# First attention of two transformer blocks: the weighing by the values in two halves of the queries, with a longer ring of exponentials

## What is computed

```python
q = _rope(proj(Wq, bq))
k = _rope(proj(Wk, bk))
v = proj(Wv, bv)
scores = jnp.einsum('bhtd,bhsd->bhts', q, k) / scale
attn = jax.nn.softmax(scores, axis=-1)
out = jnp.einsum('bhts,bhsd->bhtd', attn, v)
...
x = x + _layernorm(_L0_attn_ref(_layernorm(x, axis=-1), ...), axis=-1)
x = x + _layernorm(_L0_ffn_ref(_layernorm(x, axis=-1), ...), axis=-1)
```

## Time and profile before

| | us |
|---|---|
| median of 3 runs | 3386.52 (3385.89 to 3389.96) |
| the profiled execution | 3379.02 |
| its span, first to last instruction | 3377.2 |
| the first attention, in the span | 238 to 1638 |

### The profile page before, as it was taken

How to read it: one execution, slowest core, us unless ns; L and a number is a source line. 1 busy time by engine, 2 the same in 40 slices (tenths; PEclk the granted TensorE clock), 3 DMA queues, 4 the chain that set the end, 5 groups by cost and what they waited for, 6 DMA issues and landing times. The chain is left out here.

```text
span 3377.2 us, 56295 instructions
## 1 busy us (share of the span) xinstructions
PE 3182.4 (94%) x20728; PEld 2050.2 (61%) x20792; DVE 2572.0 (76%) x4114; ACT 2144.2 (63%) x4870; POOL 764.8 (23%) x954
## 2 busy tenths in 40 slices
PE   8979999999999999999859999999999999999996
PEld 5633333333333333333448888888888888888885
DVE  4578888888888888886357777777777777777774
ACT  3417777777777777777745555555555556565563
POOL 4500000000000000000343333333334343343341
PEclk9959999999999999999979999999999999999998
DMA  3322222222222222222400000000000000000001
GB/s 116 129 50 39 39 38 38 38 38 38 38 38 38 34 36 32 33 38 29 144 32 1 1 0 0 0 0 0 0 1 34 1 0 0 0 0 0 0 1 68
DMA packets 47027, 97.95 MB, mean 29 GB/s; under 512 B 17184, under 2 KB 29472, under 8 KB 40480
## 3 DMA queue, kind: packets, MB, share of 16 engines
q1 hardware_dynamic: 42400, 95.48, 15.1%
q10 hardware_dynamic: 4544, 1.38, 0.2%
HBM read 71.13 MB, written 25.69 MB: 29 GB/s over the span
## 5 line engine op out<-in xcount | busy, mean ns | idle before, releaser
L653 DVE TENSOR_REDUCE mx<-aux 128x1 f32<-128x1024 f32 x1024 | 1203.6, 1219 | 169.0 <-PE aux L528 168.8
L623 ACT ACTIVATE probs<-scores 128x512 f32<-128x512 f32 x2048 | 1062.9, 604 | 312.1 <-PE scores L552 308.9
L528 PE MATMUL aux<-k_stack,q_stack 48*128 48x512 f32 x2048 | 815.1, 476 | 31.6 <-DMA k_stack<-qk_dram 18.2
L552 PE MATMUL scores<-q_stack,k_stack 50*128 50x512 f32 x2048 | 756.4, 450 | 50.7 <-ACT probs L623 24.6
L552 PEld LDWEIGHTS scores<-q_stack,k_stack 50*128 50x128 f32 x2048 | 342.7, 186 | 602.6 <-ACT probs L623 549.6
L563 PE MATMUL pv<-probs,v_ones 128*32 128x512 f32 x4096 | 551.3, 610 | 1.4 <-ACT probs L623 0.7
L528 PEld LDWEIGHTS aux<-k_stack,q_stack 48*128 48x128 f32 x2048 | 345.3, 191 | 132.9 <-DVE mx L653 68.6
L1186 PE MATMUL bank<-QO,w_sb 128*128 128x128 f32 x2816 | 333.5, 278 | 0.9 <-ACT QO L1267 0.9
L1186 PEld LDWEIGHTS bank<-QO,w_sb 128*128 128x128 f32 x2816 | 321.3, 193 | 12.1 <-issue 10.3
L494 POOL CAST m_parts<-head_max 128x16 fp32r<-128x16 f32 x32 | 6.3, 196 | 1370.8 <-DVE head_max L658 1370.8
L1199 PE MATMUL bank<-kT,wqkv_sb 64*128 64x128 f32 x1984 | 288.6, 285 | 9.5 <-issue 0.4
(11 more groups left out here) (172 smaller groups left out, 4667.7 us busy)
## 6 DMA issues: line engine op xcount, KB each, us to landing
q_stack<-qk_dram SPq DMA_DIRECT2D x192, 128.0 KB, 5.0
k_stack<-qk_dram SPq DMA_DIRECT2D x192, 128.0 KB, 6.9
qk_dram<-qkT_hi SPq DMA_DIRECT2D x32, 256.0 KB, 3.1
qk_dram<-qkT_lo SPq DMA_DIRECT2D x32, 256.0 KB, 3.6
out<-x_sb SPq DMA_DIRECT2D x9, 384.0 KB, 4.1
wqkv_sb<-in_wqkv SPq DMA_DIRECT2D x2, 1536.0 KB, 7.4
w_sb<-in_w SPq DMA_DIRECT2D x2, 1408.0 KB, 11.3
x_sb<-in_x SPq DMA_DIRECT2D x1, 2048.0 KB, 18.8
```

What stands on the lines that cost most here:

```text
L528: last = nc.tensor.matmul(aux[:, ring["unit"], block_of_keys % 2], q_stack[rows, r % BODY, tile * P:(tile + 1) * P], k_stack[rows, r % BOD ...
L552: nc.tensor.matmul(scores[:, item % BANKS1], k_stack[0:SCORE_ROWS, r % BODY, s * P:(s + 1) * P], q_stack[0:SCORE_ROWS, r % BODY, j * 512:( ...
L623: nc.scalar.activation(probs[:, item % PROBS], scores[:, item % BANKS1], ACT.Exp, scale=float(D1) ** -0.5).then_inc(probs_ready, 1)
L653: nc.vector.reduce_max(mx[:, slot, tile, half:half + 1], aux[:, unit].rearrange("p a k -> p (a k)"), AX.X).then_inc(max_taken, 1)
```

## The change

`weigh` gets a half: it does the first or the last 256 queries of each block in all four matmuls, and both halves add up in the same bank. `weigh_earlier` picks the step that is meant. In a step, at j = 0 the second half of the step before last is weighed, and at j = 2 the first half of the last step, so a half stands behind every second pair. In step 1 the first half comes at j = 3 instead, since the copy of `pv` has to be done. `pv_done` rises with the second half. The ring `probs` has 12 blocks instead of 8, and the exponentials wait for the weighing three steps back. ScalarE's copy of `pv` moves behind its first exponential of step 1, because the last half of a head is now weighed at j = 0 of that step.

```diff
--- before.py
+++ after.py
@@ -337,9 +337,10 @@
 BLOCKS = T // 512
 BANKS1 = 3
 UNITS = 2
-PROBS = 8
+PROBS = 3 * BLOCKS
 BODY = 3
 VW = 32
+HALF = 256
 LEAD = 5
 AHEAD = BLOCKS * (TB + LEAD) - 1
 LOADS = 6
@@ -552,17 +553,27 @@
                 nc.tensor.matmul(scores[:, item % BANKS1], k_stack[0:SCORE_ROWS, r % BODY, s * P:(s + 1) * P],
                                  q_stack[0:SCORE_ROWS, r % BODY, j * 512:(j + 1) * 512], start=True, stop=True).then_inc(scores_ready, 1)
 
-            def weigh(r, s):
+            def weigh(r, s, half):
 
                 if s == 0:
                     pe.wait_ge(v_made, r + 1)
                     if r:
                         pe.wait_ge(pv_copied, r)
                 pe.wait_ge(probs_ready, BLOCKS * (TB * r + s + 1))
+                columns = slice(half * HALF, (half + 1) * HALF)
                 for j in range(BLOCKS):
-                    last = nc.tensor.matmul(pv[VW * j:VW * (j + 1), :], v_ones[:, r % BODY, s, :], probs[:, (BLOCKS * s + j) % PROBS],
-                                            start=(s == 0), stop=(s == TB - 1), tile_position=(0, VW * j))
-                last.then_inc(pv_done, 1)
+                    last = nc.tensor.matmul(pv[VW * j:VW * (j + 1), columns], v_ones[:, r % BODY, s, :], probs[:, (BLOCKS * (TB * r + s) + j) % PROBS, columns],
+                                            start=(s == 0 and half == 0), stop=(s == TB - 1 and half == 1), skip_group_check=True, tile_position=(0, VW * j))
+                if half == 1:
+                    last.then_inc(pv_done, 1)
+
+            def weigh_earlier(r, d, s, back, half, left, first):
+
+                if s >= back:
+                    if left >= d:
+                        weigh(r + d, s - back, half)
+                elif not first:
+                    weigh(r + d - 1, TB + s - back, half)
 
             def output_item(r):
 
@@ -581,10 +592,10 @@
                     a, tile, block_of_keys = max_item(d, s, j)
                     if left >= a:
                         score_for_max(r + a, tile, block_of_keys, head_begun if (d, s, j) == (0, LEAD, 1) else None)
-                    if j == 2 and s == 0 and not first:
-                        weigh(r + d - 1, TB - 1)
-                    elif j == 2 and s and left >= d:
-                        weigh(r + d, s - 1)
+                    if j == 0:
+                        weigh_earlier(r, d, s, 2, 1, left, first)
+                    if j == (3 if s == 1 else 2):
+                        weigh_earlier(r, d, s, 1, 0, left, first)
                     if j == 2 and (d, s) == (0, ROWS_STEP) and left >= 1:
                         maximum_rows(r + 1)
                     if j == 2 and (d, s) == (1, OUT_STEP) and not first:
@@ -618,16 +629,16 @@
             def exponentiate(r, s, j):
                 item = BLOCKS * (TB * r + s) + j
                 act.wait_ge(scores_ready, item + 1)
-                if j == 0 and TB * r + s >= 2:
-                    act.wait_ge(pv_done, TB * r + s - 1)
+                if j == 0 and item >= PROBS:
+                    act.wait_ge(pv_done, TB * r + s - PROBS // BLOCKS + 1)
                 nc.scalar.activation(probs[:, item % PROBS], scores[:, item % BANKS1], ACT.Exp, scale=float(D1) ** -0.5).then_inc(probs_ready, 1)
 
             def head(r, n, left):
                 for d, s in steps():
-                    if (d, s) == (1, 1):
-                        act.wait_ge(pv_done, TB * (r + 1))
-                        nc.scalar.copy(o_stage[:], pv[:]).then_inc(pv_copied, 1)
                     for j in range(BLOCKS):
+                        if (d, s, j) == (1, 1, 1):
+                            act.wait_ge(pv_done, TB * (r + 1))
+                            nc.scalar.copy(o_stage[:], pv[:]).then_inc(pv_copied, 1)
                         if (d, s, j) == (0, ROWS_STEP, 3) and left >= 1:
                             place = [what[3] for what in aux_items(left)].index("rows")
                             copy_rows(r + 1, (first_unit(left) + place) % UNITS)
```

## The result

| | us |
|---|---|
| before, median of 4 runs | 3386.81 (3385.89 to 3389.96) |
| changed, median of 4 runs | 3434.61 (3426.62 to 3469.98) |
| ratio | 1.016 (95% interval 1.0086 to 1.0234) |
| profiled execution, before and changed | 3379.02 and 3442.48 |

The change made the kernel slower by 1.6%, where 1.2% faster was forecast. Its runs differ by 43 us among themselves, those of before by 4 here, and by 26 in the 16 runs beside the first experiments. One run of one experiment (eight halved steps, 3526.9 us) fell into the chip's slower state and is left out of its median and ratio.

The account below looks back on a forecast made before the run. PE was taken as the pace-setter, stalled for score banks while ScalarE idled during weighings. Terms 74 + 3 - 18 - 3 - 8 - 6 - 3 gave 39 us off: 3340 profiled, 3347 median, range 3312 to 3386.

Parts of the forecast that it names:

- The regular step: Four score pairs and one weighing in the first attention: 2.61 us to become 2.46, 74 us off over 512 steps.
- the bound of PE: In the regular step after the change PE sets the pace at 2.46 us; VectorE needs 2.35, ScalarE 2.07.
- the gone wait for ScalarE: Fourth score pair held 0.39 us until ScalarE frees a score bank; this wait was to vanish.
- neither 0.50 nor 0.71: Bounds on half a weighing until the next pair: 0.50 with nothing fixed, 0.71 with the fixed part doubled; 0.57 taken.
- Rows of maxima: Step 13 of a head: maximum matmul behind the transpose waits for VectorE; +0.85 us a head, 18 us back in all.
- output: Step 3 of the next head, with the output transposes: next half +0.84 us, 3 us back in all.
- switch of heads: Step 1, where the copy of pv waits for the last half: +0.37 us, 8 us back in all.
- plain head: A head without a loop's end: 42.9 us before, forecast 41.4 after.
- The 3 us off for VectorE's end of a head: The 0.1 us left over per head before, which 0.4 us of slack should take in: 3 us off.
- The end of the loop: Every third head, the sequencer lowers the semaphores: +1.40 us before, 2.0 taken after, 6 us back over ten ends.
- The clock: Stretches at 1.2 instead of 2.4 GHz after a loop's end cost more: 3 us charged, bounds 0 and 24.
- the rival: Clock falls at each loop's end: 24 us instead of 3, giving 3368 us; chance 8%.

Follow-up runs that it names:

- the first experiments: The follow-ups told first: the changed kernel with its 32 heads written out instead of a loop, 3321.08 us; the kernel before, likewise written out, 3360.16 us.
- eight halved steps: Changed kernel in its loop, weighings of steps 3 to 10 in halves, the other eight whole, about 1982 PE instructions a turn: 3461.24 us, ratio 1.0258.
- 1694: Changed kernel in its loop, weighings of steps 6 and 7 alone in halves, about 1694 PE instructions a turn: 3364.77 us, ratio 0.9935.
- 1790: Changed kernel in its loop, weighings of steps 5 to 8 in halves, the other twelve whole, about 1790 PE instructions a turn: 3437.48 us, ratio 1.0173.
- 1646: Changed kernel in its loop, weighing of step 7 alone in halves, about 1646 PE instructions a turn: 3381.32 us, ratio 0.9999.
- loop of six heads: Kernel before, whole weighings, six heads in a turn of the loop instead of three: 3397.54 us, ratio 1.004.
- loop of 15 heads: Changed kernel, all in halves, 15 heads in a turn, so two turns and one branch back: 3341.92 us, ratio 0.9887.

## Why the prediction was wrong

The range, 3312 to 3386, did not hold 3434.61, and the sign was wrong. By its own steps:

- **The regular step**: right. 2 x (0.34 + 0.32 + 0.57) = 2.46 is in the trace, and the bound of PE, and the gone wait for ScalarE. The half cost its 0.57, neither 0.50 nor 0.71. With 1.00 for the whole, that leaves 0.14 in each that does not shrink with the columns. The Trainium skill (TensorEngine Tiling (Array Packing), Key Properties) says that a change of the tiling mode drains the engine; the trace agrees in so far as every half pays the 0.14, but no run separates a drain from other fixed costs. The multiplication was off: 512 x 0.15 is 77, not 74. The steps measure 2.609 and 2.463, which is 75, so it did no harm.
- **Rows of maxima, output, switch of heads**: right, +0.85, +0.84 and +0.38 (2.84 less 2.46), against +0.85, +0.84 and +0.37. A plain head took 41.5, 41.4 was forecast.
- **The 3 us off for VectorE's end of a head**: wrong. In the trace the step with the last item of a head is 0 to 0.45 us longer than 2.46 in a plain head, 0.1 in the mean, so the slack does not take it in. The plain heads take 41.6 in the mean, not 41.4, which makes about 7 us over 32 heads; the 41.5 of the head above is one of the shorter ones.
- **The end of the loop**: this is the step that failed. I priced it from the 3.12 us of before, as work of the sequencer that halves cover less, at 2.0, which is 6 us more for all ten. The branch back takes 3.4 to 3.9 us instead of 0.21, over the nine 30.5 us more, since a turn of 2369 PE instructions is not kept and 1598 were.
- **The clock**: the mechanism was named, its size was not. 3 us were charged, and 24 in the rival, by one step after each end. PE now idles 4.9 to 5.5 us at a taken branch where it idled 1.6, and the granted clock falls within each of these idle times and stays down for 7 to 41 us; with 7 us at the tenth end it is 181 us of the stage after its start. A half follows a half in 2.16 us there instead of 1.23. The nine ends with a taken branch took together 113 us more than plain heads; 18 of that is the 2.0 forecast, 30.5 the branches, and the 64 left is the clock.

The sum closes to a few us: the stage took from its first score to the last weighing 1400.3 us before and 1452.9 after, +52.6, where -39 was forecast, 91.6 apart. The branches are 30.5 of it. The clock cost 64 at the nine ends and about 3 at the tenth, but before had paid for it too (24 us at the lower level, 8 us by the heads that they lie in) and 3 more were charged, so it is 56. The 5 left are of the size of the plain heads' 7. Another 8 us of the profiled execution lie ahead of the stage, where both kernels run the same instructions; the start of the stage lies between 228 and 245 us in the twelve traces, in no order with the changes.

Two things in the profile should have led here. The count of PE's instructions per turn was in the prediction (32 to 48 per step), but only as a rate, never as a length. And after the first turn of the loop the trace of before has no instruction packets in the loop at all: the body is kept, so its length has a limit that the change could cross. The Trainium skill has the rule, and I did not weigh it: Runtime: NRT & Kernel Launch, Instruction fetch mechanics, says that instructions are fetched in blocks of 16 KB, in sequence, that PE's memory for them holds 2048, and that a taken branch to a target outside the current window of two blocks waits for a fetch. The traces agree on the block (155 packets, 2.54 MB) and on the wait, with the packet inside each long branch. They do not agree on the window of two blocks: before branches back over 1598 instructions in 0.21 us, without a fetch. And the limit in a loop was lower than 2048: 1694 were kept, 1790 and 1982 were not. In the first turn the kernels with 1598, 1646 and 1694 fetched seven blocks, those with 1790 and 1982 eight; so what is kept may be seven blocks of 256, an estimate from these counts that no run tests closer.

The large spread of the runs fits: how long the clock stays down differs from end to end (7 to 41 us in one execution). What decides it stays open. With whole weighings it was 7 to 14 (four ends in a loop of six heads), with halves over 20 at 15 of 28 ends; no run separates the reasons.

## What to carry to other kernels

Before you add instructions to a loop's body, count those of each engine per turn, and look in the profile whether instructions are fetched inside the loop at all: if not, the body is kept, and there is a length at which that ends. The loss then is not at the changed instructions but at the branch back, and a busy PE pays for the stall again in clock, here twice as much (64 us against 30.5). Where a forecast is right for every instruction and still misses, look at what happens once per turn; and taking the loop away is a quick way to see it: here the halves gain 39 us without the loop and lose 48 within it.

## What the runs showed of the hardware

- PE's sequencer kept a loop body of 1598, 1646 and 1694 instructions over ten turns without a fetch after the first, but not one of 1790, 1982, 2369 or 3179. The branch back took 0.21 us in the first three and 3.3 to 3.9 in the others, and in the loop of 15 heads (11777). One packet of instructions lay inside each of these 32 long branches, and ended 1.3 to 1.5 us before the branch did.
- Straight code of over 20000 PE instructions in the stage was fetched without a visible cost, at 24 matmuls and weight loads in 1.23 us: the regular step is 2.46 us written out as in the loop, and with whole weighings 2.61 in both.
- Within each of the 32 idle times of PE at these branches, 4.8 to 5.7 us long, the granted clock fell to its lower level. It stayed there for 7 to 41 us, while PE was busy again. At idle times of 1.6 us this happened two to six times in ten (four kernels whose body is kept), for 3 to 10 us. Fetching without an idle time, in straight code, did not bring it down; an idle time of 5 us without a fetch is in no run.
